# Mask bias as a row of the folded query side, instead of a bias product ahead of each half tile of scores

## The reference

```python
x = x + tanh(g_xattn) * xattn(layernorm(x), ctx, mask, Wq, Wk, Wv, Wo)   # x: (4, 256, 256), ctx: (4, 64, 128)
x = x + tanh(g_ffn) * ffn(layernorm(x), gate_w, w1, w3, w2, sw1, sw3, sw2)

# xattn: 16 query heads of 128, 8 key and value heads
scores = einsum('bhtd,bhsd->bhts', q, k) / sqrt(128)
scores = where(mask, scores, -inf)              # one mask value for each batch entry and context token
attn = nan_to_num(softmax(scores))
out = einsum('bhts,bhsd->bhtd', attn, v)        # then @ Wo
# ffn: softmax over 4 experts, the best 2 of each token, SwiGLU experts, and one shared SwiGLU expert
```

## Time and profile before

| | |
|---|---|
| median of three runs | 240.26 us |
| the profiled execution | 241.17 us, of which its span 239.4 us |
| TensorE busy | 218.5 us (91%) |
| VectorE busy | 150.8 us (63%) |
| GpSimd busy | 130.7 us (55%) |
| ScalarE busy | 118.9 us (50%) |
| granted TensorE clock, mean | 0.992 |

### The profile page before, as it was taken

One profiled execution on the slowest core, in us unless ns is written; L12 is line 12 of the kernel. 1 busy time (PEld: TensorE's weight loads), 2 busy tenths in 40 slices (PEclk: granted clock), 3 DMA queues, 4 the chain that ended last, 5 costly groups with the idle time before them and its releaser, 6 DMA issues.

```text
span 239.4 us, 4751 instructions
## 1 busy us (share of the span) xinstructions
PE 218.5 (91%) x1490; PEld 187.4 (78%) x1490; DVE 150.8 (63%) x333; ACT 118.9 (50%) x244; POOL 130.7 (55%) x121
## 2 busy tenths in 40 slices
PE   2999999999999999977897999999999999999930
PEld 2877677788899999965776879888898889888930
DVE  0499979999978989757978694373333333333310
ACT  3477768637946566655634423453334533443220
POOL 3226222463799999857649924456554655453222
PEclk9999999999999999999999999999999999999996
DMA  6835438022122344322013402222333234322322
GB/s 228 267 117 179 150 110 274 37 66 66 66 90 92 129 156 153 98 85 84 22 45 105 139 3 34 57 45 48 50 65 63 44 48 64 68 44 25 38 30 23
DMA packets 12919, 20.99 MB, mean 88 GB/s; under 512 B 2048, under 2 KB 7808, under 8 KB 12896
## 3 DMA queue, kind: packets, MB, share of 16 engines
q1 hardware_dynamic: 9104, 15.45, 19.9%
q0 software_dynamic: 3648, 4.98, 12.7%
q10 hardware_dynamic: 144, 0.26, 0.3%
HBM read 16.10 MB, written 4.59 MB: 86 GB/s over the span
## 4 chain that ended last, share of the span: by engine, by line
PE 55%; DMA 23%; DVE 9%; issue 6%; ACT 4%; POOLq 1%; SPq 0%; ACTq 0%; DVEq 0%
DMA out_dram<-probs,tok 20%; PE bankR L362 5%; PE bankP L243 5%; PE bankQ L243 4%; PE bankP L245 4%; PE bankP L244 4%; PE bankQ L244 4%; PE bankQ L245 4%; PE bankS L243 3%; PE bankS L244 3%; PE bankS L245 3%; PE bankR L409 3%; DVE spot L1112 2%; PE bankP L339 2%; ACT probs L816 2%
## 5 line engine op out<-in xcount | busy, mean ns | idle before, releaser
L1446 POOL DMA_INDIRECT out_dram<-probs,tok x19 | 30.1, 1584 | 46.3 <-ACT probs L816 25.6
L1418 POOL TENSOR_TENSOR reg<-raw,reg 128x768 fp32r<-128x768 f32 x16 | 29.5, 1845 | 5.7 <-ACT reg L770 5.5
L1437 POOL DMA_INDIRECT probs<-x2d,tok x19 | 20.5, 1079 | 9.0 <-issue 8.1
L243 PE MATMUL bankS<-reg,hT 128*128 x76 | 21.6, 284 | 1.9 <-DVE hT L1219 1.9
L1386 POOL TENSOR_TENSOR w_lo<-raw,w_hi 128x512 fp32r<-128x512 f32 x8 | 10.4, 1297 | 23.4 <-ACT w_hi L694 23.4
L1219 DVE TENSOR_TENSOR hT<-bankR,hT 128x512 fp32r<-128x512 f32 x19 | 13.1, 691 | 15.3 <-ACT hT L800 15.2
L816 ACT ACTIVATE probs<-bankS,wgt_tab 128x256 f32<-128x256 f32 x14 | 6.6, 473 | 32.1 <-DMA out_dram<-probs,tok 22.6
L244 PE MATMUL bankS<-reg,hT 128*128 x76 | 21.6, 284 | 0.0
L245 PE MATMUL bankS<-reg,hT 128*128 x76 | 21.5, 283 | 0.0
L1210 DVE TENSOR_TENSOR gT_lo<-bankS,gT_hi 128x256 fp32r<-128x256 f32 x19 | 8.0, 423 | 21.4 <-ACT gT_hi L790 21.4
L1399 POOL TENSOR_TENSOR probs<-probs,rcp 128x1024 f32<-128x1024 f32 x8 | 15.3, 1908 | 4.8 <-DVE rcp L1012 4.6
(11 more groups left out here) (232 smaller groups left out, 697.2 us busy)
## 6 DMA issues: line engine op xcount, KB each, us to landing
raw<-ffn_dram SPq DMA_DIRECT2D x18, 384.0 KB, 3.3
raw<-kvq_dram SPq DMA_DIRECT2D x6, 384.0 KB, 3.2
probs<-wo_dram SPq DMA_DIRECT2D x8, 256.0 KB, 2.7
x_sb<-x_dram SPq DMA_DIRECT2D x1, 1024.0 KB, 5.8
x2d<-xn SPq DMA_DIRECT2D x8, 128.0 KB, 1.7
out_dram<-x_sb SPq DMA_DIRECT2D x8, 128.0 KB, 1.7
probs<-x2d,tok POOLq DMA_INDIRECT x19, 2.8
out_dram<-probs,tok POOLq DMA_INDIRECT x19, 3.8
```

The lines of the kernel that those rows point to most:

```text
L243: eng.matmul(acc, l_hi, r_hi, start=start, stop=False, **kw)
L1418: pool.tensor_tensor(lo, raw[:, (m + 2) % RS, :], hi.bitcast(F32), ALU.subtract).then_inc(wf_lo, 1)
L1437: pool.indirect_dma_start(out=x_blk[:, i % 4, :], out_offset=None, in_=x2d[:, :], in_offset=bass.IndirectOffsetOnAxis(ap=tok[:, i:i + 1], ...
L1446: pool.indirect_dma_start(out=out[:, :], out_offset=bass.IndirectOffsetOnAxis(ap=tok[:, i:i + 1], axis=0), in_=y_blk[:, i % 4, :], in_offs ...
```

## The change

The first input column of the query weights is taken off all the columns (a layernormed row sums to zero, so the scores stay as they are). The folded query side then has a row of zeros for input column 0. The normalized x gets a one in column 0, and the bias is written into the freed row of the high part. The product with `onerow` goes.

Done by whom: GpSimd makes the negated first column of each head's weights (`nfirst`, 128x2), ScalarE's rounding copy of 128x512 becomes two activations of 128x256 with that column as bias, GpSimd makes the unrounded difference (`wsub`, 128x512) before the low part, and after it copies the bias into the row (`bias_row`, one partition, 512 values, eight times). GpSimd's loop over the groups is written out.

```diff
@@ TensorE
+                if b == 0:
+                    pe.wait_ge(one_ok, 1)          # in turn_x
...
-                pe.matmul(acc, onerow[:, :], bias[:, b * S:(b + 1) * S].unsqueeze(1).to_broadcast([P, NH // 2, S]),
-                          start=True, stop=False)
...
-                                False, k == KD - 1)
+                                k == 0, k == KD - 1)
...
-            pe.wait_ge(onerow_ok, 1)
-            pe.wait_ge(bias_ok, 1)
...
+            pe.wait_ge(row_ok, NG // 2)
             scores_half(0, 0).then_inc(sc_half, 1)
+            pe.wait_ge(row_ok, NG)
             scores_half(0, 1).then_inc(sc_ps, 1)
@@ ScalarE
-                act.copy(w_hi[:, s, 0:2 * D], raw_kvq[:, s, 2 * HD:KVQ]).then_inc(wq_hi, 1)
+                act.wait_ge(nfirst_ok, g + 1)
+                for hh in range(2):
+                    ins = act.activation(w_hi[:, s, hh * D:(hh + 1) * D], raw_kvq[:, s, 2 * HD + hh * D:2 * HD + (hh + 1) * D],
+                                         ACT.Identity, bias=nfirst[:, s, hh:hh + 1])
+                ins.then_inc(wq_hi, 1)
...
-                    act.activation(xn0[:, n % TPB, :], xtile(n), ACT.Identity, bias=mrneg[:, n:n + 1],
+                    act.activation(xn0[:, n % TPB, 1:], x_sb[:, n * D + 1:(n + 1) * D], ACT.Identity, bias=mrneg[:, n:n + 1],
@@ VectorE
-                dve.wait_ge(prep, 2)
+                dve.wait_ge(prep, 1)
                 dve.tensor_scalar(bias[:, :], mask_f[:, :], -1.0, MASKED, ALU.add, ALU.mult).then_inc(bias_ok, 1)
...
+                dve.wait_ge(prep, 2)
+                dve.memset(xn0[:, :, 0:1], 1.0).then_inc(one_ok, 1)
...
-            dve.memset(onerow[:, :].bitcast(F32), 0.0).then_inc(prep, 1)
-            dve.wait_ge(prep, 1)
-            dve.memset(onerow[0:1, :].bitcast(F32), 1.0).then_inc(onerow_ok, 1)
@@ GpSimd
-            def split_wq(g, s):
+            def split_wq(g, s, n):
+                pool.wait_ge(kvq_ld[s], (n + 1) * 16)
+                pool.tensor_scalar(nfirst[:, s, :], raw_kvq[:, s, 2 * HD:KVQ].rearrange("p (h d) -> p h d", d=D)[:, :, 0], -1.0, None,
+                                   ALU.mult).then_inc(nfirst_ok, 1)
+                wait(pool, wq_lo, g)
+                w = raw_kvq[:, s, 2 * HD:KVQ].rearrange("p (h d) -> p h d", d=D)
+                pool.tensor_tensor(wsub.rearrange("p (h d) -> p h d", d=D), w, w[:, :, 0:1].to_broadcast([P, 2, D]),
+                                   ALU.subtract).then_inc(wsub_ok, 1)
+                pool.wait_ge(wsub_ok, g + 1)
                 pool.wait_ge(wq_hi, g + 1)
-                pool.tensor_tensor(w_lo[:, s, 0:2 * D], raw_kvq[:, s, 2 * HD:KVQ], w_hi[:, s, 0:2 * D].bitcast(F32),
-                                   ALU.subtract).then_inc(wq_lo, 1)
+                pool.tensor_tensor(w_lo[:, s, 0:2 * D], wsub, w_hi[:, s, 0:2 * D].bitcast(F32), ALU.subtract).then_inc(wq_lo, 1)
+
+            def bias_row(g):
+
+                pool.wait_ge(a_lo, g * 2 + 2)
+                pool.tensor_copy(A_hi[0:1, 0, :, bass.ds(g * 2 * S, 2 * S)].rearrange("p b (a s) -> p b a s", s=S),
+                                 bias[0:1, :].rearrange("p (b s) -> p b s", s=S).unsqueeze(2).to_broadcast([1, NB, 2, S])).then_inc(row_ok, 1)
...
             for s in range(2):
-                split_wq(s, s)
+                split_wq(s, s, 0)
             pool.wait_ge(mhalf_ok, 1)
+            pool.wait_ge(bias_ok, 1)
             for s in range(2):
-                split_wq(2 + s, s)
+                split_wq(2 + s, s, 1)
+                bias_row(s)
             finish_x(0)
-            with pool.Fori(2, NG // 2) as it:
+            for it in range(2, NG // 2):
                 for s in range(2):
-                    split_wq(it * 2 + s, s)
+                    split_wq(it * 2 + s, s, it)
+                    bias_row(it * 2 + s - 2)
+            bias_row(NG - 2)
+            bias_row(NG - 1)
             finish_x(1)
```

More of the change, by code:

```diff
@@ L82, in build @@
         bias_at = nc.sbuf_base - NB * S * 4
-        onerow = sb("onerow", [P, P], F32R)
+        nfirst = sb("nfirst", [P, 2, 2])
         anyvalid = sb("anyvalid", [P, NB])
@@ L184, in build @@
         mask_f = xn0[:, 0, :]
+        wsub = xn2[:, :, :].rearrange("p a n -> p (a n)")
         first_tile = probs[:, 0, :].rearrange("p (a n) -> p a n", a=2)
@@ L209, in build @@
         prep = sem("prep")
-        onerow_ok, tg_ok, made_ok = sem("onerow_ok"), sem("tg_ok"), sem("made_ok")
+        tg_ok, made_ok = sem("tg_ok"), sem("made_ok")
         gwhi_ok, gwlo_ok = sem("gwhi_ok"), sem("gwlo_ok")
         kv_ps, k_hi, kv_sb = sem("kv_ps"), sem("k_hi"), sem("kv_sb")
+        nfirst_ok, wsub_ok, row_ok, one_ok = sem("nfirst_ok"), sem("wsub_ok"), sem("row_ok"), sem("one_ok")
         wq_hi, wq_lo = sem("wq_hi"), sem("wq_lo")
@@ L1264, in _ @@
             dve.wait_ge(tg_ok, 1)
-            dve.wait_ge(prep, 3)
+            dve.wait_ge(prep, 2)
             dve.tensor_scalar(tga[:, :], anyvalid[:, :], tg[:, 0:1], None, ALU.mult)
```

## The result

Over 17 runs each, the changed kernel took 242.52 us (median; 240.68 to 244.39) and the kernel before 240.44 us (239.15 to 244.44). The ratio is 1.0071, with a 95% interval of 1.0042 to 1.0100: slower by 1.0 to 2.4 us, where 1.4 us faster was forecast, and the median is outside the forecast's range (237.0 to 241.0). The ratios leave out the few slow runs, over 1.5 % above a kernel's fastest, and differ by up to 0.2 % from the quotient of two medians.

The account below looks back on a forecast made before the run. TensorE was taken to bound the kernel, with VectorE nearly as full. First stage 0.7 us later less 2.1 us gained in the attention gave -1.4 us, against the median of 240.26: 238.9 us, range 237.0 to 241.0.

Parts of the forecast that it names:

- 16 x 0.232 = 3.7 us, the most that the removal can give: Attention: sixteen bias products on TensorE's chain, 0.232 us each, as upper bound of the gain.
- rival A: Attention: VectorE gives way and TensorE gets the products' 3.7 us in full; 237.1 us, chance 17%.
- 0.7 of 2.3 us up to `attend(1, 0)`: Attention, tiles 0 to 4: ten products take 2.3 us, but VectorE's idle time lets only 0.7 through.
- The 0.14 us I left out: VectorE's idle time before the maximum at 50.36, not counted because the following difference may wait for GpSimd's scaling.
- These six count in full, and nothing is late next: Attention, tiles 5 to 7: six products behind `attend(1, 0)` gain 1.4 us, with 1.8 us of slack at VectorE's low part.
- First stage: 0.55 + 0.15 = 0.7 us later: First stage: 0.55 us from the mask's bias wait, 0.15 from ScalarE's added work and late load; bounds 0 and 4.4.
- Rival B: First stage: GpSimd sets the pace at 4.75 us a group, 4.4 us late; 242.6 us, chance 17%.
- So do the 19 expert blocks: After 92 us: routing and expert blocks move along with the end of the attention, passing its gain on.
- The prediction's own signs: Trace marks for right (bias about 0.3 us, group 3 query side about 22.7) or wrong (later than 23.5, row above 1.2).

Follow-up runs that it names:

- e4: Kernel before without the sixteen bias products and nothing put in their place, so the mask's bias is left out; 240.88 us, ratio 0.9993.
- e5: e4 with sixteen small unread products added on TensorE ahead of `turn_x2(5)`; 239.85 us, ratio 0.9970 to the kernel before.
- e9: Changed kernel with the sixteen bias products put back, the new first stage kept; 242.19 us, ratio 1.0075 to the kernel before.
- e1: Changed kernel measured again without any edit; 242.84 us, ratio 1.0101 to the kernel before.
- e2: Changed kernel with one early 128x1 activation on ScalarE, so its table loads during the first transfer; 241.79 us, ratio 1.0046 to the kernel before.
- e6: Changed kernel with sixteen small unread products added on TensorE ahead of `turn_x2(5)`; 242.26 us, ratio 1.0059 to the kernel before.
- e8: e2 (table loaded early) with sixteen small unread products added on TensorE; 240.13 us, ratio 1.0000 to the kernel before.
- e10: Changed kernel with negated keys and weights, no `nfirst`, table early, GpSimd's bias wait later, sixteen small products; 240.31 us, ratio 0.9999 to the kernel before.
- e12: Kernel before with 20 small unread products added on TensorE ahead of `turn_x2(5)`; 241.21 us, ratio 1.0013.
- e7: Kernel before with eleven small unread products added on TensorE ahead of `turn_x2(5)`; 240.57 us, ratio 1.0017.
- e11: e4 with 31 small unread products added on TensorE ahead of `turn_x2(5)`; 240.97 us, ratio 1.0011 to the kernel before.

## Why the prediction was wrong

**"16 x 0.232 = 3.7 us, the most that the removal can give":** nothing speaks against it as a bound, and rival A, TensorE gets it all, is refuted by e4 and e5, whose intervals end at 0.9 and 1.3 us of gain.

**"0.7 of 2.3 us up to `attend(1, 0)`": right.** From the first maximum to `add_attention(0)` it was 19.86 us and is 18.98, 0.9 us shorter, about the 0.85 of idle time that I had counted. The other traces repeat it: 19.8 to 19.9 us in the four kernels with the products, 19.0 in the ten without. The 0.14 us I left out came, and the 128x8 difference took 0.28 longer, ending at 52.14 with GpSimd's scaling.

**"These six count in full, and nothing is late next": this step failed.** From `add_attention(0)` to `add_attention(4)` it was 27.07 us and is 26.86, where 1.4 less were forecast: 0.2 us. In the other traces it is 27.0 to 27.1 with the products and 26.9 without, and the rest of the attention, up to `add_attention(7)`, falls from 17.3 to 17.1 or 17.2, so that the six gave about 0.3 us in all. I looked at one hand-over, at 70 us, and measured its slack against TensorE, taking for granted that what made VectorE wait would move along. It was GpSimd, through ScalarE: the weights' splits, the scaling and the small operations for the layernorm follow each other without a gap (9.72 of 10 us), ScalarE's order puts the rounding of the probabilities behind its wait for `mrneg`, and VectorE waits for that. GpSimd paced these tiles in the kernel before already: its share from 70 to 80 us was as high, a window that I had not put among the rows, and its scalings of the probabilities start 6.9 us apart there (77.30, 84.22, 91.09) and 6.9 apart in the changed kernel (76.59, 83.49, 90.38). That the removal's worth was 0.9 us and not 2.1 is shown by B - A, and by e5's interval (0.1 to 1.3). That GpSimd is what held back the rest is read from the chain and from this period; no run took work off GpSimd to test it.

**"First stage: 0.55 + 0.15 = 0.7 us later": too small, 1.8 us by e9 (1.1 to 2.5).** Its terms were near. The bias took 0.29 us with GpSimd idle (0.28 taken), VectorE's low keys started at 15.94 (16.15), the query side of group 3 at 22.45 (22.7 expected), `wsub` took 1.04 (1.3), the row 0.60 (0.8), the two activations 0.91 (1.0). Rival B, GpSimd as pacemaker of the first stage, did not occur: it sat idle between its operations, 3.1 us ahead of group 2 and 2.2 ahead of group 7's low part among them. (In B's price 43.5 less 39.18 is 4.3 us, not 4.4.) The sum has no term for the table load, which went from ScalarE's idle start to between the arrival of the weights and their rounding. Loading it early gave 1.3 us (e1 to e2) and 1.4 us (e6 to e8) by the ratios, with intervals of 1.4 and 1.1 us around them. With it early, what is left of the first stage is 0.7 us (e8 against e5, intervals overlapping), the forecast's figure.

The traces do not show the table load as a loss, though. The first output side starts at 10.43 to 10.59 in the five with the late load, at 9.87 to 10.86 in the six with the old first stage, and at 9.39 to 9.95 in the three with the early load: early loading is ahead of the late one by half a microsecond or more, but the late load is level with five of the six old ones. A is 41.4 to 42.2, 40.6 to 42.4 and 40.7 to 41.2 in the same three groups. That the late load costs anything against the kernel before rests on the times alone, and how the 1.8 us divide between it, the added work and the instruction transfer at 22 us is open.

**"So do the 19 expert blocks" move with the end of the attention: wrong in the last five.** They moved up to the fourteenth scatter. Behind it an instruction transfer fell into a scatter, 0.3 to 1.9 us in C - B. That it is the place of the code is supported by the match of long scatters and transfers in all traces, by the absence of long scatters behind 205 us in all four kernels with sixteen products (e5, e6, e8, e10), by the times of e5 against e4 and e8 against e2, lower by 0.6 and 1.1 us though within overlapping intervals, and by e12's trace. Only the runs with sixteen products brought the transfers where they were meant to go; e7, e11 and e12 each missed. It isn't settled in size: e7, e11 and e12 can't be told from the kernel before by their times, and e6 gained 0.3 to 1.0 us.

The sum by measurements: first stage +1.8, products -0.7 (e5) to -0.9, code +0.3 to +1.1 (e6, e5, e8 against their twins), in all +1.2 to +2.2, against +1.7 measured (1.0 to 2.4). Each term has an interval of about 1 us, so that the agreement is a weak check.

The prediction's own signs did not warn. Those of being right came: no L389, the bias at 0.29 us, the query side of group 3 at 22.45, TensorE's waits for VectorE ahead of `attend(1, 0)`; the first scores started at 43.4, not 43.8. None of being wrong did: 22.45 is under 23.5, the row's 0.60 under 1.2, GpSimd was idle between 24 and 40 us, and TensorE waited before 92 us. None of them looked at the tiles behind `attend(1, 0)`, at the table or at the scatters.

## What to carry to other kernels

Before an operation's slack counts as free, follow its wait one engine further back: a window in which a third engine is at 97% will take the gain whoever the chain names now. An engine's one-time set-up belongs where it still waits for nothing; after an edit to an engine's first instruction or to the waits ahead of it, look where that set-up went. Where serial transfers end a kernel, compare kernels up to the first of these and behind it separately, before explaining a median: a change of the instruction count alone can move a code transfer into them.

## What the runs showed of the hardware

A 16 KB instruction transfer that started 1.9 to 3.2 us behind the start of a scatter of 128 rows made it 4.5 to 5.5 us long instead of 3.6, eleven times out of twelve; one that started within 1.6 us of the scatter's start, 3.2 us or more behind it, or between two, left it at 3.4 to 4.0. One that started at 21.5 to 22.7 us, beside a transfer of 384 KB issued at about 22 us, went with 3.8 to 4.8 us to landing instead of 3.1 to 3.6. GpSimd's difference with a broadcast second input took 1.04 us for 128x512, against 1.26 to 1.29 with a full one, and its copy of 512 values on one partition 0.60. TensorE's first query side ran at 0.12 us a matmul wherever it started at 8.8 us or later, and where it started at 7.6 to 8.1 from one to all of its matmuls were followed at 0.21 us or more, with a granted clock of 1.00 throughout.
